# A two-layer graph network on one core: the gate's bias off TensorE, masks and output products in another order, first loads and products later

## The chip, the core and the metric

One core of a Trainium2 chip (trn2). The metric is the device time of one launch in microseconds, the median of several runs; lower is better. PE is TensorE, ACT ScalarE, DVE VectorE, POOL GpSimd, SP the engine that only issues transfers.

## The reference, cut to what matters

64 batches of 128 nodes with 384 features, `x` of 64 x 128 x 384, and a mask `adj` of 64 x 128 x 128. First a masked attention with 6 heads of 64, then a layer norm, then a graph attention with 12 heads of 32, a gate, and a second layer norm:

```python
# layer 0, per batch
q, k, v = x @ Wq + bq, x @ Wk + bk, x @ Wv + bv
probs = softmax(q k^T / 8 + where(mask, 0, -9e15))      # 6 heads
x1 = layernorm(x + (probs v) @ Wf + bf)
# layer 1, per batch
h = x1 @ W                                              # 12 heads
src, dst = tanh(h) . w_src, tanh(h) . w_dst
attn = softmax(where(adj, leaky_relu(src + dst^T), -999))
f = elu(attn h + b)
gate = sigmoid(x1 @ H_w^T + H_b)
out = layernorm(x1 + gate * f + (1 - gate) * x1)
```

## The kernel before, in words

Every projection is a split product (`split_product`, L250): both factors are held as a rounded high part and a remainder, and for each of the three chunks of 128 rows three products are added up (hi hi, lo hi, hi lo), so nine matmuls of 384 or 512 columns. In the trace all of them have line L254 and differ by tiles: `wq`, `wk`, `wv` (q, k, v of four batches at once), `wf` (output), `w` (h) and `hw` (gate). The gate's product ends with a tenth matmul (L429) that adds the bias: `ones_b` times `hb_rows`, in which the bias lies in three bf16 parts. ScalarE reads the finished sum from PSUM and stores the tangent of its half (L672); VectorE uses it two batches later (L846).

The work is written out by hand. Each engine has its own loop over 18 groups `n`, with four steps `j` each, and the order in the text is the order on the engine; semaphores tie them together. In a step three batches are under way: `ta` in the attention, `tl = ta - 2` in the first half of the graph layer ("gat"), `tl - 1` in its softmax and product ("tail"), and `tl - 2` in gating and second norm. Beside them the projections of the next group are made in four portions (`fill_a`, `fill_b`). "First batch" below is one with j = 0, "fourth batch" one with j = 3, in which v is projected. Group 0 has projections alone; group 16 has attention without projections; group 17 finishes the graph layer.

TensorE's step (L488 to L536): scores of `ta` (L355); turn f (L485); turn x1 (L410); a portion of projections; h; a second portion; turn p0 (L363); gate chunk 0; turn the exponentials of four heads (L467); context (L383); gate chunk 1; four more heads; gate chunk 2 and the bias (L429); output chunks 0 and 1; turn the six small columns `sd` (L435, L436); the last four heads; output chunk 2; the logits (L449), three matmuls in three banks of `ps_d`; the mask of the next batch's scores (L345), two bf16 matmuls into `ps_s`; the product with h (L477, "apply"). The logits wait for `rows_L` (ScalarE, L680) and `cols_R` (VectorE, L911).

VectorE's step, as far as it is near: copy p0T's odd half (L852), h with its bias (L860), the sums `sd` (L866), one evacuation of q, k or v, `ctxT_lo` (L747), then sd split into three bf16 parts by five small instructions (L892 to L902), a copy of four turned heads (L765), `cols_R` (L911), and the end of the second residual with its statistics (L920).

ScalarE's step: x1T_hi (L612), exponentials of the scores (L621), an evacuation, in fourth batches also the rounding of the next x (L558), elu's exponential (L638), tanh of h (L644), exponentials of heads 0 to 3 (L592), p0T's even half (L655), heads 4 to 7, ctxT_hi (L663), heads 8 to 11, the gate (L672), copies of turned heads (L604), rows_L, the three parts of z (L690), and fT (L696).

GpSimd's step: the mask added to z in three parts (L1000, up to batch 57; from batch 58 on TensorE adds it, L454, and VectorE sums the exponentials, L773), the multiply of p0 by the inverse sums (L1029), tanh(h) times the two weight rows (L1037), the two normalisations (L986 to L991), and two of x with bias (L978) or of the remainder of x (L945).

At the start SP issues x, four weights, the constants and two more weights, each weight into a staging buffer; ScalarE's queue issues the two small biases, the identity and the adjacency (1 MB, as bytes, turned into the bf16 `mask` by POOL, L962). After the projections of group 0 TensorE multiplies bv with Wf (`bias_product`, L323, in fp32), VectorE splits the gate's bias (L727 to L736), a transfer of POOL moves it to `hb_rows`, and VectorE adds bf to make `bf_all` (L881); the first mask of the scores waits for that.

## Time and profile before

| what | value |
|---|---|
| median of the runs shown | 1112.39 us (1108.36 to 1113.97, 3 runs) |
| the profiled execution | 1113.29 us |
| its span, first to last instruction | 1111.3 us |
| mean granted clock of TensorE | 0.986 |
| instructions | 25345 |

The profile is one execution. "Idle before" is the time that an engine stood still just before an instruction, with the name of what ended it. Matmuls are pipelined, so the time between the starts of two neighbours is what one costs, and its duration is longer. In timelines neighbours of one kind are merged, with their count behind an x.

### The profile page before, as it was taken

How to read it: one execution, taken by the hardware profiler on the slowest of the kernel's cores; microseconds unless marked ns; L12 is line 12 of the kernel's file. 1: busy time of each engine (PE TensorE's matmuls, PEld its weight loads, DVE VectorE, ACT ScalarE, POOL GpSimd, SP SyncE). 2: the span in 40 equal slices, each digit the busy share in tenths (PEclk: the TensorE clock that was granted, in tenths of full speed). 3: DMA queues.
4: the chain of work that ended last, by engine and by line, in shares of the span. 5: the costliest groups of instructions: out<-in, count | busy, mean ns of one | idle time of the engine just before them, and what ended most of it. 6: DMA issues, size and time to landing. Idle time of an engine off the chain costs nothing.

```text
span 1111.3 us, 25345 instructions
## 1 busy us (share of the span) xinstructions
PE 1055.4 (95%) x8318; PEld 883.4 (79%) x8318; DVE 916.6 (82%) x1844; ACT 878.1 (79%) x3183; POOL 748.0 (67%) x893
## 2 busy tenths in 40 slices
PE   5889999999999999999999999999999999997774
PEld 4678888888888888888888888888888888886552
DVE  4447888888888888888888888889888888988986
ACT  3348888888888888888888888888888888888754
POOL 1467777676777677677767768776776877665323
PEclk9999999999999999999999999999999999999986
DMA  9101002010200201020020102002020200100000
GB/s 273 59 2 58 16 9 73 16 65 16 71 17 9 72 15 65 16 72 17 9 73 15 65 16 72 16 8 73 16 71 10 72 15 9 44 16 15 9 15 29
DMA packets 25892, 44.65 MB, mean 40 GB/s; under 512 B 2462, under 2 KB 23714, under 8 KB 25762
## 3 DMA queue, kind: packets, MB, share of 16 engines
q1 hardware_dynamic: 23234, 41.91, 11.2%
q10 hardware_dynamic: 2496, 1.12, 0.5%
q8 instruction: 68, 1.11, 0.4%
q14 instruction: 62, 0.51, 0.2%
q0 software_dynamic: 32, 0.00, 0.0%
HBM read 30.43 MB, written 12.58 MB: 39 GB/s over the span
## 4 chain that ended last, share of the span: by engine, by line
PE 87%; issue 6%; POOL 4%; DVE 2%; ACT 1%; DMA 1%; POOLq 0%; ACTq 0%; DVEq 0%
PE ps_b L254 22%; PE ps_d L254 17%; PE ps_a L254 13%; PE ps_d L467 7%; PE ps_s L355 5%; PE ps_a L383 4%; PE ps_c L477 4%; PE ps_s L363 4%; PE ps_d L449 3%; PE ps_c L485 3%; PE ps_s L345 2%; PE ps_b L410 2%; POOL thw L1037 1%; PE ps_d L429 1%; POOL s L989 1%
## 5 line engine op out<-in xcount | busy, mean ns | idle before, releaser
L592 ACT ACTIVATE z<-z,s 128x128 f32<-128x128 f32 x696 | 270.0, 394 | 0.0
L1000 POOL TENSOR_TENSOR z<-z,mask 128x512 f32<-128x512 f32 x174 | 197.6, 1164 | 62.8 <-ACT z L690 62.8
L1029 POOL TENSOR_TENSOR p<-p,s 128x768 f32<-128x768 f32 x64 | 94.2, 1472 | 168.7 <-DVE s L823 168.7
L621 ACT ACTIVATE p<-ps_s,s 128x128 f32<-128x128 f32 x384 | 135.3, 374 | 12.0 <-DVE s L789 11.9
L592 ACT ACTIVATION_READ_ACCUMULATOR z<-z,s 128x1 f32 x696 | 135.3, 194 | 0.0
L1037 POOL TENSOR_TENSOR thw<-th,w_sd 128x768 f32<-128x768 f32 x64 | 117.6, 1837 | 18.7 <-ACT th L644 18.7
L467 PE MATMUL ps_d<-ident,z 128*128 128x128 f32 x768 | 117.6, 276 | 5.4 <-ACT z L595 5.2
L690 ACT ACTIVATE z<-ps_d 128x512 f32<-128x512 f32 x192 | 100.8, 597 | 25.7 <-PE ps_d L449 19.7
L467 PEld LDWEIGHTS ps_d<-ident,z 128*128 128x128 f32 x768 | 90.1, 142 | 13.0 <-ACT z L595 7.1
L852 DVE COPY p0T<-ps_s 128x384 f32<-128x384 f32 x64 | 35.7, 558 | 71.3 <-PE ps_s L363 71.3
L612 ACT ACTIVATE x1T_hi<-ps_b 128x384 fp32r<-128x384 f32 x64 | 31.5, 492 | 74.1 <-PE ps_b L410 74.1
L604 ACT ACTIVATE p1T<-ps_d 128x512 f32<-128x512 f32 x128 | 76.0, 594 | 14.4 <-PE ps_d L467 14.3
L254 PE MATMUL ps_d<-hw_hi,x1T_hi 128*128 128x384 f32 x192 | 82.1, 428 | 0.0
L621 ACT ACTIVATION_READ_ACCUMULATOR p<-ps_s,s 128x1 f32 x384 | 81.9, 213 | 0.0
L254 PE MATMUL ps_b<-wf_hi,ctxT_hi 128*128 128x384 f32 x192 | 78.6, 409 | 2.7 <-DVE ctxT_lo L747 1.3
L989 POOL TENSOR_TENSOR s<-s,minus_half 128x1 f32<-128x1 f32 x128 | 72.3, 565 | 10.7
L817 DVE TENSOR_REDUCE s<-z 128x8 f32<-128x1024 f32 x64 | 77.3, 1208 | 0.0
L254 PE MATMUL ps_d<-w_hi,x1T_hi 128*128 128x384 f32 x192 | 66.0, 344 | 7.0 <-DVE x1T_lo L747 7.0
L945 POOL TENSOR_TENSOR xT_lo<-x_cols,xT_hi 128x768 fp32r<-128x768 f32 x30 | 58.8, 1980 | 16.9 <-DVE sd_parts L902 9.4
L789 DVE TENSOR_REDUCE s<-ps_s 128x6 f32<-128x768 f32 x64 | 60.4, 944 | 10.6 <-PE ps_s L355 10.3
L978 POOL TENSOR_TENSOR xb<-xb,bf_all 128x768 f32<-128x768 f32 x32 | 58.5, 1828 | 11.9 <-DVE sd_parts L902 10.1
L254 PE MATMUL ps_d<-w_lo,x1T_hi 128*128 128x384 f32 x192 | 65.3, 340 | 0.0
(160 smaller groups left out, 3429.7 us busy)
## 6 DMA issues: line engine op xcount, KB each, us to landing
x_cols<-in_xT_dram SPq DMA_DIRECT2D x16, 768.0 KB, 6.3
xb<-in_x_dram SPq DMA_DIRECT2D x16, 768.0 KB, 4.9
out_dram<-y SPq DMA_DIRECT2D x64, 192.0 KB, 1.9
z<-in_L_gnn_Wq_dram SPq DMA_DIRECT2D x1, 576.0 KB, 6.9
p1T<-in_L_gnn_Wk_dram SPq DMA_DIRECT2D x1, 576.0 KB, 9.3
qT<-in_L_gnn_Wv_dram SPq DMA_DIRECT2D x1, 576.0 KB, 11.8
kT<-in_L_gnn_Wf_dram SPq DMA_DIRECT2D x1, 576.0 KB, 13.9
z<-in_L_gnn_W_dram SPq DMA_DIRECT2D x1, 576.0 KB, 12.1
```

The lines of the kernel that those rows point to most:

```text
L254: last = pe.matmul(out_ap, lhs(a, c), rhs(b, c), start=(c == 0 and k == 0), stop=(closed and c == C - 1 and k == 2))
L467: last = pe.transpose(ps_d[:, q, (a % 4) * N:(a % 4 + 1) * N], z[:, a, :], ident[:])
L592: done = act.activation(z[:, a, :], z[:, a, :], ACT.Exp, bias=neg1[:, a:a + 1], accum_out=sum1[:, a:a + 1])
L604: act.activation(p1T[:, 4 * q:4 * q + 4, :], ps_d[:, q, :].rearrange("p (a n) -> p a n", a=4), ACT.Copy).then_inc(S[f"p1T_{q}"], 1)
L621: last = act.activation(p0[:, o, i, :], ps_s[:, o, i * N:(i + 1) * N], ACT.Exp, bias=neg0[:, k:k + 1], accum_out=sum0[:, k:k + 1])
L690: act.activation(z[:, 4 * q:4 * q + 4, :], ps_d[:, q, :].rearrange("p (a n) -> p a n", a=4), ACT.Prelu, alpha=0.2).then_inc(S["z_ready"], 1)
L789: dve.tensor_reduce(neg0.rearrange("p (o i) -> p o i", o=2), ps_s[:, :, 0:C * N].rearrange("p o (i n) -> p o i n", i=C), AX_X, ALU.max, ne ...
L817: dve.tensor_reduce(neg1[:, 0:8], z[:, 0:8, :], AX_X, ALU.max, negate=True).then_inc(S["neg1_ready"], 1)
L989: pool.tensor_tensor(rs, ve, minus_half[:], ALU.pow).then_inc(S[small], 1)
L1000: pool.tensor_tensor(z[:, 4 * q:4 * q + 4, :], z[:, 4 * q:4 * q + 4, :], mask[:, t, :].unsqueeze(1).broadcast_to([P, 4, N]), ALU.add).then ...
L1029: pool.tensor_tensor(p0[:].rearrange("p o i n -> p (o i) n"), p0[:].rearrange("p o i n -> p (o i) n"), inv0.unsqueeze(2).broadcast_to([P, ...
L1037: pool.tensor_tensor(thw[:], th[:].unsqueeze(1).broadcast_to([P, 2, D]), w_sd[:], ALU.mult).then_inc(S["thw_ready"], 1)
```

## The change

- The gate's bias leaves TensorE. The matmul L429 goes, with `ones_b`, `hb_rows`, their splitting on VectorE and the transfer. The bias is loaded once as 128 equal rows (`hb_all`, 192 KB). ScalarE copies the gate's sum plain from PSUM; in the next step GpSimd adds the bias, behind its masks of z and ahead of the multiply of p0; then ScalarE takes the tangent, in place, ahead of p0T's even half.
- TensorE's order: the mask of the next batch's scores goes from behind the logits to before the output projection, and of that projection only chunk 0 stays before the turn of sd; chunks 1 and 2 follow the last turned heads.
- ScalarE's order: fT is made between the first and the second part of z, not behind the third.
- The bound from which VectorE sums the exponentials goes from batch 58 to 61; up to there ScalarE's exponentials bring their sums along. The masks stay where they were.
- At the start: the adjacency is issued by SP ahead of the fourth weight; `bias_product` comes behind the first scores and writes `ps_c`, and `bf_all` follows on VectorE behind the first maxima; the wait for it goes from the first mask to the first turn of sd. The bf16 identity is made a step earlier, and x of group 0 gets its bias behind the first multiply of p0.

```diff
 UNFILLED = G * (NG - 1) - LAG
+UNATTENDED = B - LAG - 1
...
             for n, name in enumerate(W_ORDER):
+                if n == 3:
+                    sp.dma_start(adj_u8, adj_dram).then_inc(S["adj_in"], 16)
...
-                    sp.dma_start(hb_row, Hb.rearrange("(o d) -> o d", o=1)).then_inc(S["const_in"], 16)
+                    sp.dma_start(hb_all[:], Hb.partition_broadcast(P)).then_inc(S["const_in"], 16)
...
-                        last = pe.matmul(ps_s[:, 0, 0:D], bv_col[:, c:c + 1].broadcast_to([P, P]),
+                        last = pe.matmul(ps_c[:, 0:D], bv_col[:, c:c + 1].broadcast_to([P, P]),
                                          w_parts["wf"][k][:, c, :].bitcast(F32), start=(c == 0 and k == 0),
                                          stop=(c == C - 1 and k == 1))
...
-                    pe.wait_ge(S["bf_ready"], 1)
...
             def project_gate(chunks):
 
-                split_product(ps_d[:, 2, 0:D], lambda a, c: x1T[a][:, c, :],
-                              lambda b, c: w_parts["hw"][b][:, c, :], chunks, closed=False)
+                last = split_product(ps_d[:, 2, 0:D], lambda a, c: x1T[a][:, c, :],
+                                     lambda b, c: w_parts["hw"][b][:, c, :], chunks)
                 if chunks[-1] == C - 1:
-
-                    pe.matmul(ps_d[:, 2, 0:D], ones_b[:], hb_rows[:], start=False, stop=True
-                              ).then_inc(S["gate_made"], 1)
+                    last.then_inc(S["gate_made"], 1)
 
             def turn_sd(t):
 
                 pe.wait_ge(S["sd3_ready"], t + 1)
+                if t == 0:
+                    pe.wait_ge(S["bf_ready"], 1)
                 pe.transpose(ps_rows, sd_rows, ident_b[:]).then_inc(S["sd_turned"], 1)
                 pe.transpose(ps_cols, sd_cols, ident_b[:]).then_inc(S["sd_turned"], 1)
 
             def logits(t):
 
                 pe.wait_ge(S["h_ready"], t + 1)
-                pe.wait_ge(S["gate_ready"], t + 1)
+                pe.wait_ge(S["gate_moved"], t + 1)
                 pe.wait_ge(S["rows_ready"], t + 1)
                 pe.wait_ge(S["cols_ready"], t + 1)
...
                         scores(g, 1 - par, j)
+                        if ta == 0:
+                            bias_product()
...
-                    if n == 0 and j == 3:
-                        bias_product()
...
-                    if att:
-                        project_out(ta, g, j, n, (0, 1))
-                    if gat:
-                        turn_sd(tl)
-                    if tail:
-                        turn_p1(tl - 1, gat, (2,))
-                    if att:
-                        project_out(ta, g, j, n, (2,))
-                    if gat:
-                        logits(tl)
                     if 0 <= ta and ta + 1 < B:
                         scores_mask(ta + 1)
+                    if att:
+                        project_out(ta, g, j, n, (0,))
+                    if gat:
+                        turn_sd(tl)
+                    if tail:
+                        turn_p1(tl - 1, gat, (2,))
+                    if att:
+                        project_out(ta, g, j, n, (1, 2))
+                    if gat:
+                        logits(tl)
                     if tail:
                         apply_p1(tl - 1, (j + 1) % 2, gat)
             pipeline(pe, iteration)
...
-            act.dma_start(adj_u8, adj_dram).then_inc(S["adj_in"], 16)
...
-                        if t < UNFILLED:
+                        if t < UNATTENDED:
...
+                def product_f(t):
+
+                    act.wait_ge(S["ph_made"], t + 1)
+                    if due(t):
+                        act.wait_ge(S["f_turned"], t)
+                    act.activation(fT[:], ps_c[:, 0:D].rearrange("p (c n) -> p c n", c=C),
+                                   ACT.Copy).then_inc(S["fT_ready"], 1)
...
+                    if tail:
+                        act.wait_ge(S["gate_biased"], tl)
+                        act.activation(gate[:, (tl - 1) % 3, :], gate[:, (tl - 1) % 3, :], ACT.Tanh,
+                                       scale=0.5).then_inc(S["gate_ready"], 1)
                     if att:
                         act.wait_ge(S["p0_turned"], ta + 1)
...
-                        act.activation(gate[:, tl % 3, :], ps_d[:, 2, 0:D], ACT.Tanh,
-                                       scale=0.5).then_inc(S["gate_ready"], 1)
+                        act.activation(gate[:, tl % 3, :], ps_d[:, 2, 0:D], ACT.Copy).then_inc(S["gate_moved"], 1)
...
                             act.activation(z[:, 4 * q:4 * q + 4, :], ps_d[:, q, :].rearrange("p (a n) -> p a n", a=4),
                                            ACT.Prelu, alpha=0.2).then_inc(S["z_ready"], 1)
-                    if tail:
-                        act.wait_ge(S["ph_made"], tl)
-                        if due(tl - 1):
-                            act.wait_ge(S["f_turned"], tl - 1)
-                        act.activation(fT[:], ps_c[:, 0:D].rearrange("p (c n) -> p c n", c=C),
-                                       ACT.Copy).then_inc(S["fT_ready"], 1)
+                            if q == 0 and tail:
+                                product_f(tl - 1)
+                    elif tail:
+                        product_f(tl - 1)
             pipeline(act, iteration)
...
+                    if ta == 0:
+                        dve.wait_ge(S["bvf_made"], 1)
+                        dve.tensor_tensor(bf_all[:], ps_c[:, 0:D], bf_in, ALU.add).then_inc(S["bf_ready"], 1)
...
+                        dve.wait_ge(S["gate_ready"], t2 + 1)
...
+                    if n == 0 and j == 2:
+                        dve.wait_ge(S["ident_in_ready"], 16)
+                        dve.tensor_copy(ident_b[:], ident[:]).then_inc(S["consts_ready"], 1)
                     if n == 0 and j == 3:
                         small_constants()
-                        dve.wait_ge(S["bvf_made"], 1)
-                        dve.tensor_tensor(bf_all[:], ps_s[:, 0, 0:D], bf_in, ALU.add).then_inc(S["bf_ready"], 1)
                     if att:
...
-                pool.wait_ge(S["hb_small"], 5)
-                pool.wait_ge(S["padding_ready"], 1)
-                pool.dma_start(hb_rows[0:3, :], hb_split[:]).then_inc(S["hb_moved"], 16)
...
                     if tail:
                         z_mask(tl - 1)
+                    if tail:
+                        pool.wait_ge(S["gate_moved"], tl)
+                        if tl == 1:
+                            pool.wait_ge(S["const_in"], 16 * 7)
+                        pool.tensor_tensor(gate[:, (tl - 1) % 3, :], gate[:, (tl - 1) % 3, :], hb_all[:], ALU.add
+                                           ).then_inc(S["gate_biased"], 1)
...
                     if ta == 0:
+                        xb_with_bias(0, 0, slice(0, 2))
+                        xb_with_bias(0, 0, slice(2, 4))
                         moved_constants()
...
-                    if n == 0 and j == 3:
-                        xb_with_bias(g, par, slice(0, 2))
-                        xb_with_bias(g, par, slice(2, 4))
```

## Rows read from the trace of the kernel before

**Rows 1.** Page, busy time of each engine over the span.

```profile
PE 1055.4 (95%) x8318; PEld 883.4 (79%) x8318; DVE 916.6 (82%) x1844; ACT 878.1 (79%) x3183; POOL 748.0 (67%) x893
```

**Rows 2.** Timeline of PE, one batch (start, duration, engine, line, operation, tiles, count, idle before).

```profile
574.69 0.34 PE L254 MATMUL ps_d<-hw_lo,x1T_hi 128*128 128x384 f32 x1
574.87 0.34 PE L429 MATMUL ps_d<-hb_rows,ones_b 128*128 128x384 bf16 x1
...
575.21 0.33 PE L254 MATMUL ps_b<-wf_hi,ctxT_lo 128*128 128x384 f32 x1
...
576.10 0.22 PE L435 MATMUL ps_c<-ident_b,sd_parts 128*96 128x128 bf16 x1
...
577.00 0.34 PE L254 MATMUL ps_b<-wf_lo,ctxT_hi 128*128 128x384 f32 x1
577.35 0.54 PE L449 MATMUL ps_d<-cols_R,rows_L 32*128 32x512 bf16 x3
577.82 0.50 PE L345 MATMUL ps_s<-mask,ident_b 128*128 128x384 bf16 x2
578.25 0.86 PE L477 MATMUL ps_c<-p1T,h 128*32 128x128 f32 x24
```

**Rows 3.** Timeline of DVE, the same batch.

```profile
575.72 0.18 DVE L902 CAST sd_parts<-sd_rest 128x24 bf16<-128x24 f32 x1
...
576.41 0.69 DVE L911 TENSOR_TENSOR cols_R<-ps_a,of_slot 96x512 bf16<-96x512 bf16 x1
```

**Rows 4.** Waits over the span (total, times, longest).

```profile
POOL p L1029 <- DVE s L823: 168.7, 64, 9.4
...
ACT p0T L655 <- PE ps_s L363: 40.6, 50, 2.2
```

**Rows 5.** Timeline of all engines, a fourth batch.

```profile
604.32 0.85 ACT L558 ACTIVATE xT_hi<-x_cols 128x768 fp32r<-128x768 f32 x1 [0.78 <-PE ps_b L254]
...
605.07 0.48 ACT L655 ACTIVATE p0T<-ps_s 128x384 f32<-128x384 f32 x1
...
605.78 0.88 PE L383 MATMUL ps_a<-p0T,v 128*64 128x128 f32 x12
...
607.56 0.56 DVE L747 TENSOR_TENSOR ctxT_lo<-ps_a,ctxT_hi 128x384 fp32r<-128x384 f32 x1 [0.30 <-ACT ctxT_hi L663]
...
608.09 0.66 POOL L991 TENSOR_SCALAR x<-r,s 128x384 f32<-128x384 f32 x1
...
608.24 0.55 DVE L894 TENSOR_TENSOR sd_rest<-sd,sd_parts 128x24 f32<-128x24 f32 x1
...
609.25 0.18 DVE L902 CAST sd_parts<-sd_rest 128x24 bf16<-128x24 f32 x1
```

**Rows 6.** Timeline of DVE, an earlier fourth batch: the cast at the same place.

```profile
90.88 0.61 DVE L892 CAST sd_parts<-sd 128x24 bf16<-128x24 f32 x1
```

**Rows 7.** Timeline of POOL, a first batch, and its multiply of the next.

```profile
613.41 3.41 POOL L1000 TENSOR_TENSOR z<-z,mask 128x512 f32<-128x512 f32 x3
617.36 1.47 POOL L1029 TENSOR_TENSOR p<-p,s 128x768 f32<-128x768 f32 x1 [0.54 <-DVE s L823]
```

**Rows 8.** Timeline of PE, the start of the attention.

```profile
32.23 0.81 PE L329 MATMUL ps_s<-wf_hi,bv_col 128*128 128x384 f32 x2
...
37.41 0.48 PE L345 MATMUL ps_s<-mask,ident_b 128*128 128x384 bf16 x2 [1.14 <-DVE bf_all L881]
...
43.84 0.88 PE L363 MATMUL ps_s<-ident,p 128*128 128x128 f32 x6 [0.78 <-POOL p L1029]
...
47.66 0.41 PE L254 MATMUL ps_b<-wf_hi,ctxT_hi 128*128 128x384 f32 x1 [1.29 <-issue]
```

**Rows 9.** Timeline of DVE, the start: the fifth weight.

```profile
23.47 1.23 DVE L718 CAST w_hi<-z 128x1152 fp32r<-128x1152 f32 x1 [0.63 <-DMA z<-in_L_gnn_W_dram]
```

**Rows 10.** Timeline of PE, a batch without projections.

```profile
1028.79 0.40 PE L449 MATMUL ps_d<-cols_R,rows_L 32*128 32x512 bf16 x3 [0.18 <-issue]
```

**Rows 11.** Timeline of ACT, the three parts of z and what follows fT.

```profile
577.76 1.57 ACT L690 ACTIVATE z<-ps_d 128x512 f32<-128x512 f32 x3 [0.31 <-PE ps_d L449]
...
580.83 0.49 ACT L612 ACTIVATE x1T_hi<-ps_b 128x384 fp32r<-128x384 f32 x1 [1.11 <-PE ps_b L410]
```

**Rows 12.** Busy time by stretch, the end (PE, PEld, DVE, ACT, POOL, PEclk, DMA share, GB/s).

```profile
1074.00:1084.00 10.00, 7.92 (x45) 5.86 (x43) 6.52 (x13) 4.36 (x10) 0.65 (x1) 0.51 0.00 0
```

More of the change, by code:

```diff
@@ L87, in build_program @@
         w_sd = sb("w_sd", [P, 2, D])
-        hb_rows = sb("hb_rows", [P, D], BF16)
+        hb_all = sb("hb_all", [P, D])
         mask = sb("mask", [P, B, N], BF16)
@@ L522, in iteration @@
                         project_gate((2,))
+                    if 0 <= ta and ta + 1 < B:
+                        scores_mask(ta + 1)
                     if att:
-                        project_out(ta, g, j, n, (0, 1))
+                        project_out(ta, g, j, n, (0,))
                     if gat:
@@ L902, in iteration @@
                         dve.tensor_copy(part[2], sd_rest[:, 1]).then_inc(S["sd3_ready"], 1)
-                    if tail and tt >= UNFILLED:
+                    if tail and tt >= UNATTENDED:
                         sum_exponentials(tt, 0)
@@ L913, in iteration @@
                                           ).then_inc(S["cols_ready"], 1)
-                    if tail and tt >= UNFILLED:
+                    if tail and tt >= UNATTENDED:
                         sum_exponentials(tt, 1)
```

37 lines of the change are left out of this document (8 added, 29 removed).

## The prediction

> **What bounds the kernel now.** I read the page first: PE is busy for 95% of the span, DVE 82%, ACT 79%, POOL 67% [rows 1]. One would take PE for the bound and every product saved for time saved. So the next view is PE's timeline of one batch in the steady part, beside DVE's. The reader is to look at starts, since a matmul's 0.34 is mostly pipeline: neighbours of 384 columns start 0.17 to 0.18 apart. PE runs without a gap except at one place: the last product of the output projection starts at 577.00, the logits could follow at 577.18, and they start at 577.35 [rows 2]. They wait for cols_R, which DVE ends at 577.10 [rows 3]. DVE is busy without a gap from the copy of p0T (L852) to there. So PE is the bound from the transposes of p0 onwards and again after the logits; between them, DVE's chain p0T, h, sums, evacuation, ctxT_lo, five small splits, cols_R is almost level with it. The batches repeat with a period of 15.6 us (first, second and third of a group of four) and about 17.75 us (fourth to first).
>
> **The removed bias product.** It costs PE 0.52 - 0.35 = 0.17 us: from the last gate product at 574.69 to the second output product at 575.21 there are 0.52, where two more products would be 0.35 [rows 2]. Over 64 batches that would be 11 us, if nothing else waited.
>
> **The new order on PE.** The two mask products cost 0.43 behind the logits (577.82 to 578.25), of which 0.32 are 2 x 384 columns; the other 0.11 is the passage from bf16 to the fp32 products, which now follows the logits directly. Ahead of the output projection they cost 2 x 0.17 = 0.34. Of that projection only one chunk (three products, 0.53) is ahead of the turn of sd instead of two. PE reaches the turn 0.17 - 0.34 + 0.53 = 0.36 earlier than 576.10, so at 575.74. But DVE ends the last split at 575.72 + 0.18 = 575.90 [rows 3], and PE can start some 0.05 later, at 575.95. The turn is thus only 0.15 earlier: **DVE's splits take the place of cols_R as the wait.** From the turn to the logits there were 1.08 without the gap (576.10 to 577.18), and now one chunk more, 1.61: logits at 577.56, after cols_R (577.10) and no longer waiting for it. The following apply (L477) comes 0.47 + 0.11 later, at 578.14 instead of 578.25. The gain in a second or third batch is 0.11 to 0.13 us, not the 0.17 + 0.17 = 0.34 that PE alone would give.
>
> **ScalarE's extra tangent** is one operation of 128x384: 0.48 long, the next one starting 0.10 before its end, so 0.38 per batch. In three batches of four ACT waits 0.70 us for the transposes of p0, and the tangent is hidden there (over the kernel that wait sums to 40.6 us in 50 batches) [rows 4]. In the fourth it is not: ACT waits for the v product instead, then rounds x (L558) and takes up p0T at 605.07 with no idle time before it, 0.15 after DVE [rows 5]. The tangent goes right between. p0T's even half then ends at 605.93 instead of 605.55; the context product (605.78) starts about 0.3 later; ctxT_hi comes 0.38 later, and ctxT_lo on DVE starts at 607.93 instead of 607.56. The first split then comes at 608.41, inside GpSimd's normalisation (608.09 to 608.75).
>
> Here the trace shows a collision: the split at 608.24 took 0.55, until GpSimd's operation ended, where its kind takes 0.18 [rows 5]. That the cast before it is held too is shown by an earlier batch, 0.61 for 0.17 [rows 6]. I let the cast wait until 608.79; the last split ends at 609.65 instead of 609.43, +0.22; in the batches in which it now ends 0.18 earlier it is +0.40. I take +0.31 for the turn of sd and, less 0.02 from the order, **+0.29 per fourth batch**. The Trainium skill (SBUF — State Buffer, on who interferes with whom) says that the pair of ports shared by VectorE and GpSimd is an exclusive lock for the whole instruction, for operations with two SBUF inputs or in a two-port mode. If only the two-input split were held and not the cast, the split would be released at the same 608.79 as now and the fourth batch would lose nothing.
>
> **GpSimd's extra add** isn't in the trace. Its nearest row is the mask addition, 3 of 128x512 in 3.41, 1.13 each [rows 7]; three quarters of that is 0.85. From below, a one-input operation of 128x384 takes 0.66 [rows 5]; from above 1.13. It stands before the multiply of p0, for which POOL waits in all 64 batches, 168.7 us in sum [rows 4], least in a first batch: 0.54 [rows 7]. There the multiply comes 0.3 later; 617.36 + 1.47 + 0.3 = 619.13 is still 0.7 ahead of PE's transposes (7.34 after the scores at 612.47). But POOL's later normalisation also comes 0.3 later and holds DVE's last split instead of the one before: the turn of sd stays where it was, and a first batch gains 0. In no other batch is it seen.
>
> **Sum over the 14 groups of the steady part:** 0 - 0.12 - 0.12 + 0.29 = +0.05 each; I take **0**.
>
> **The start.** PE now does six bias products from 32.23 to 36.1, then idles until 37.41, because DVE splits the gate's bias into three and only then makes bf_all. Afterwards come mask, scores (1.28 together) and the first fill. In the new order mask and scores start at 32.2 and the 3.9 us of bias products hide the softmax: the fill starts 1.3 earlier, the wait of 0.78 before the transposes goes, and the mask product hides in the wait of 1.29 before the output projection (0.43), in the second batch again (0.43) [rows 8]. With 0.4 for the third and fourth batch that is -3.3. The adjacency moves from ACT's queue to SP's ahead of the fourth weight, and the bias becomes a broadcast of 192 KB instead of 1.5: DVE already waits 0.63 for the fifth weight [rows 9], and a later one delays k and PE. The first weights come earlier, so I charge +0.3, between -0.5 and +2. GpSimd adds the xb bias (two of 1.83) after p0, long before it is read. **Start: -3.0.**
>
> **The drained part** (four batches without projections, period 15.45) is a chain of latencies. The logits wait 0.18 there too, at 13.26 after the scores at 1015.53 [rows 10]; sums of exponentials leave DVE, the mask leaves the chain: -0.35, -0.53, -0.53, -0.39, **-1.8**. Three last batches: the tangent lies before the last transposes once (+0.38), two bias products are gone (-0.34): **0**.
>
> **The exchange of z and fT on ACT.** fT is now made after the first of three z's, which start about 0.5 apart (three in 1.57) [rows 11], but it waits for the apply product, which ends near 579.05. z's third part so ends about 1.3 later, near 580.6; ACT was idle 1.11 before 580.83, so it fits; without that cover the exponentials of attention would come later by what exceeds it. POOL's masks in a second batch end at 582.4 and the add at 583.3, before the multiply at 583.94.
>
> **Sum:** -3.0 + 0 - 1.8 + 0 = -4.8 against the profiled execution's 1113.29 us (span 1111.3 and 2.0 around it): 1108.5. That execution is 0.9 above the median of the runs shown, 1112.39; I predict 1108.5 us, 0.35% below that median. This measurement can hardly tell less than 0.5%, 5.6 us, from nothing.
>
> **Rivals.** (1) *The DVE chain gives way* (36%): if the cast is not held in the fourth batch (-0.31) or the last split slips through in the first (up to -0.35), a group gains 0.35 to 0.9 and the time is 1096 to 1104. At its far end PE alone decides: 56 x 0.34 = 19 us and 5 at the ends, 1089. For it: PE has no other wait. Against: in the rows DVE has no slack to give. By the lock as the Trainium skill states it, whoever starts first holds the pair, and the cast may or may not be in a mode that needs it; the two cases lie 0.31 x 14 = 4.3 us apart. (2) *GpSimd becomes late in first batches* (12%). The add and DVE's two-input operations hold each other, and it takes about 2 us instead of 0.85. The multiply of p0 then ends 1.4 late, at 620.3, after PE wants it (619.81), and th's product (L1037) and the sums on DVE behind it as well: about 1.0 per group, 14 us, 1108.5 + 14 = 1122. It decides from an add of 1.5 us on (0.54 of wait and 0.9 of lead used up). For it: two-input operations do meet there. Against it: the masks of twice its columns keep to 1.13 in the same place. (3) *The gain at the start is eaten by the later loads* (10%): the fifth weight 3 us late, 1111.5. (4) The clock: at the end 10 us ran at a granted 0.51, the 1.2 GHz level, after PE had waited on DVE and ACT [rows 12]; if that stretch moves, 3 us of PE's work there change by half, so 2 to 3 us either way; it widens the range of every case.
>
> **Numbers.** The forecast case has 42%, its own range 1104 to 1113; a quarter of it lies under 1106.8. Faster by over 0.5%: 0.9 x 36 + 10 = 42. Slower by over 0.5%: 12. Within: 46. The range leaves out the far end of the first rival and most of the second: 1098 to 1115.
>
> **What would show it.** In the changed profile: the turn of sd right behind DVE's last split and the logits no longer 0.25 behind cols_R; periods near 15.5 for second and third batches, 17.9 or more from the fourth to the first; ACT's p0T copy 0.38 later in fourth batches only; the add near 0.85; scores at 32.6 instead of 37.8. Periods of 15.3 and 17.4 would prove the first rival right and my DVE chain wrong; PE waiting for POOL before the transposes of p0 in the steady part, the second.

## The result and the profile after

| | before | after |
|---|---|---|
| median of six runs each, us | 1110.51 (1108.07 to 1113.97) | 1101.91 (1100.91 to 1103.01) |
| ratio after to before | | 0.9923 (95%: 0.9901 to 0.9944) |
| the profiled execution and its span, us | 1113.29, 1111.3 | 1102.09, 1100.3 |
| mean granted clock | 0.986 | 0.989 |

The change makes the kernel 0.8% faster. The forecast was 1108.5, 4.8 us under the profiled execution of before; it came out 11.2 under it (8.6 by the medians: the profiled execution of before is 2.8 above its kernel's median). So the time lies in the range, but the gain is more than twice the one that the steps gave, and it came from elsewhere: 1101.9 is below the forecast case's own 1104 and inside the first rival's 1096 to 1104. A table of the scores' starts shows where. I group the 64 batches by their place in the group of four; a period is the time from one batch's first score to the next one's, averaged over batches 8 to 58 of the one profiled execution. The last three rows and the one of the fifth batch add up to the whole.

| | forecast | before | after | difference |
|---|---|---|---|---|
| first score of all | 32.6 | 37.82 | 37.09 | -0.73 |
| first score of the fifth batch | -3.0 | 95.39 | 95.83 | +0.44 |
| first batch, period | 0 | 15.63 | 15.27 | -0.36 |
| second | -0.12 | 15.61 | 15.34 | -0.27 |
| third | -0.12 | 15.62 | 15.42 | -0.20 |
| fourth | +0.29 | 17.76 | 17.93 | +0.17 |
| fifth to 61st batch, sum | 0 | 904.72 | 895.05 | -9.67 |
| 61st to 64th (drained; the forecast is for four periods, these are three) | -1.8 | 46.33 | 45.58 | -0.75 |
| from the last score on | 0 | 64.9 | 63.8 | -1.0 |

+0.44, -9.67, -0.75 and -1.0 make -11.0, what the spans differ by. Nearly all came from the steady part, for which the forecast was nothing; the start, for which it was -3.0, brought nothing.

The 95.39 of before is not a clean number. From 61 to 64 us of its span the granted clock was 0.53; the second and third periods are 13.05 and 15.03, where a kernel with the same start (the product off alone, below) has 11.96 and 14.60 at 1.00, and reaches the fifth batch at 93.97. Against about 94 the changed start is some 1.9 us slower, not 0.4.

From the page after: the busy times, and the group of the new add (partitions x elements, count, busy, mean ns, idle before).

```profile
PE 1040.9 (95%) x8254; PEld 874.7 (79%) x8254; DVE 900.6 (82%) x1830; ACT 909.5 (83%) x3282; POOL 812.3 (74%) x954
...
L1024 POOL TENSOR_TENSOR gate<-gate,hb_all 128x384 f32<-128x384 f32 x64 | 68.0, 1062 | 0.7 <-ACT gate L680 0.7
```

PE has lost 14.5 us of work and is busy for 95% as before [rows 1]; that share told nothing of the gain. The add takes 1.06 in the mean, not 0.85.

The waits after (total, times, longest):

```profile
POOL p L1028 <- DVE s L819: 82.2, 50, 8.3
...
PEld ps_c L432 <- DVE sd_parts L900: 19.5, 47, 1.5
...
ACT p0T L663 <- PE ps_s L361: 16.4, 46, 2.2
```

The second line is the wait that the forecast named: PE at the turn of sd now waits for DVE's last split in 47 batches. POOL has half its slack before the multiply left (82.2 us in sum, where it was 168.7), and ACT 0.36 instead of 0.81 each before p0T, the room that the tangent took [rows 4].

**A second batch after**, the same one as in [rows 2, 3, 11]; its scores began at 558.85. First PE, then DVE, POOL and ACT (start, duration, engine, line).

```profile
571.34 0.26 PE L432 MATMUL ps_c<-ident_b,sd_parts 128*96 128x128 bf16 x1
...
573.08 0.39 PE L446 MATMUL ps_d<-cols_R,rows_L 32*128 32x512 bf16 x3
573.40 0.86 PE L474 MATMUL ps_c<-p1T,h 128*32 128x128 f32 x24
```

```profile
570.62 0.45 DVE L897 TENSOR_TENSOR sd_rest<-sd_rest,sd_parts 128x24 f32<-128x24 f32 x1
571.11 0.18 DVE L900 CAST sd_parts<-sd_rest 128x24 bf16<-128x24 f32 x1
...
571.80 0.68 DVE L909 TENSOR_TENSOR cols_R<-ps_a,of_slot 96x512 bf16<-96x512 bf16 x1
```

```profile
570.38 0.66 POOL L984 TENSOR_SCALAR x<-r,s 128x384 f32<-128x384 f32 x1
```

```profile
573.50 0.60 ACT L697 ACTIVATE z<-ps_d 128x512 f32<-128x512 f32 x1 [0.77 <-PE ps_d L446]
574.33 0.49 ACT L600 ACTIVATE fT<-ps_c 128x384 f32<-128x384 f32 x1 [0.23 <-PE ps_c L474]
```

The turn of sd (571.34) follows the last split (571.11 + 0.18) by 0.05, as forecast, and cols_R is done at 572.48, 0.60 before the logits: it is no longer the wait. The fourth of DVE's five small operations is held until POOL's normalisation ends (570.38 + 0.66). What differs from the forecast stands behind the turn. The logits come 1.74 after it, not 1.61: the last output product starts at 572.81, and from it to the bf16 logits there are 0.27 where I had counted 0.17. The apply comes 0.32 after the logits, not 0.58.

**A first batch after**, scores at 607.54: POOL, DVE.

```profile
611.95 1.02 POOL L1024 TENSOR_TENSOR gate<-gate,hb_all 128x384 f32<-128x384 f32 x1
...
619.60 0.66 POOL L984 TENSOR_SCALAR x<-r,s 128x384 f32<-128x384 f32 x1
```

```profile
619.53 0.18 DVE L900 CAST sd_parts<-sd_rest 128x24 bf16<-128x24 f32 x1
```

The add moves POOL's whole sequence back, and its normalisation now begins 0.07 after the last split has begun: the split is through in 0.18. The turn of sd then starts at 619.82, 12.28 after the scores, against 12.49 in a second batch.

**A fourth batch after**, scores at 589.61, all engines, beside [rows 5]:

```profile
599.28 0.85 ACT L554 ACTIVATE xT_hi<-x_cols 128x768 fp32r<-128x768 f32 x1 [0.78 <-PE ps_b L253]
600.03 0.51 ACT L657 ACTIVATE gate<-gate 128x384 f32<-128x384 f32 x1
600.45 0.47 ACT L663 ACTIVATE p0T<-ps_s 128x384 f32<-128x384 f32 x1
...
601.02 0.88 PE L381 MATMUL ps_a<-p0T,v 128*64 128x128 f32 x12 [0.21 <-issue]
...
602.93 0.56 DVE L740 TENSOR_TENSOR ctxT_lo<-ps_a,ctxT_hi 128x384 fp32r<-128x384 f32 x1 [0.70 <-ACT ctxT_hi L671]
603.04 0.67 POOL L984 TENSOR_SCALAR x<-r,s 128x384 f32<-128x384 f32 x1
603.40 0.34 DVE L890 CAST sd_parts<-sd 128x24 bf16<-128x24 f32 x1
...
604.42 0.18 DVE L900 CAST sd_parts<-sd_rest 128x24 bf16<-128x24 f32 x1
```

The tangent lies before p0T, the context begins 0.28 later than before (11.40 after the scores instead of 11.12, means of the fourth batches), and the cast at 603.40 is held to 603.74, when POOL's operation has ended. The last split is done 14.99 after the scores instead of 14.68: the +0.31 of the forecast.

**The start after**: SP's issues, then DVE, then PE, then the window from 31.0 on (PE, PEld, DVE, ACT, POOL, PEclk, DMA share, GB/s).

```profile
3.19 0.83 SPq L198 DMA_DIRECT2D x<-in_adj_dram  x1
4.06 11.93 SPq L209 DMA_DIRECT2D kT<-in_L_gnn_Wf_dram  x1
...
19.41 0.43 SPq L209 DMA_DIRECT2D z<-in_L_gnn_W_dram  x1
```

```profile
27.42 0.76 DVE L723 CAST w_hi<-z 128x1152 fp32r<-128x1152 f32 x1 [4.08 <-DMA z<-in_L_gnn_W_dram]
...
29.49 0.74 DVE L750 TENSOR_SCALAR kT<-ps_b,bk_col 128x512 f32<-128x512 f32 x1
```

```profile
30.29 0.44 PE L253 MATMUL ps_b<-wv_hi,xT_hi 128*128 128x384 f32 x1 [2.07 <-DVE kT L750]
...
37.09 0.94 PE L353 MATMUL ps_s<-kT,qT 64*128 64x128 f32 x12
```

```profile
31.00:34.40 3.40, 3.40 (x13) 3.40 (x12) 1.99 (x3) 0.85 (x1) 0.42 (x1) 0.50 0.13 54
```

The issue of Wf (the fourth weight), the next on SP's queue behind the adjacency, lasts 11.93 us, and what follows it is issued 6 to 12 us later than before: the fifth weight (W, staged in z) reaches DVE 4 us later [rows 9], DVE's evacuation of k stands behind it, PE waits 2.07 for that, and after the gap it runs 3.4 us at a granted 0.50, the 1.2 GHz level (its products start 0.32 apart instead of 0.17); from 34.4 on it is back at full clock. The first score comes at 37.09 instead of the 32.6 forecast.

### The profile page after: what moved, and what is told of

Read it like the earlier page. It is cut to its first block, busy times and chain, and to the rows that moved or that the text cites. A ratio compares the mean times of both kernels' runs of the same rounds, so it can differ in the third digit from the quotient of the medians.

```text
span 1100.3 us, 25365 instructions
## 1 busy us (share of the span) xinstructions
PE 1040.9 (95%) x8254; PEld 874.7 (79%) x8254; DVE 900.6 (82%) x1830; ACT 909.5 (83%) x3282; POOL 812.3 (74%) x954
## 4 chain that ended last, share of the span: by engine, by line
PE 75%; DVE 10%; issue 8%; POOL 4%; SPq 2%; ACT 1%; DMA 1%; POOLq 0%; DVEq 0%
PE ps_b L253 20%; PE ps_d L253 13%; PE ps_a L253 13%; PE ps_d L464 5%; PE ps_s L353 5%; PE ps_c L474 4%; PE ps_s L361 4%; PE ps_c L482 3%; DVE sd L863 2%; PE ps_a L381 2%; PE ps_b L408 2%; PE ps_d L446 2%; DVE kT L750 2%; DVE h L857 1%; DVE sd_rest L897 1%
## 5 line engine op out<-in xcount | busy, mean ns | idle before, releaser
L588 ACT ACTIVATE z<-z,s 128x128 f32<-128x128 f32 x732 | 284.4, 399 | 0.0
L1028 POOL TENSOR_TENSOR p<-p,s 128x768 f32<-128x768 f32 x64 | 94.2, 1473 | 82.2 <-DVE s L819 82.2
L697 ACT ACTIVATE z<-ps_d 128x512 f32<-128x512 f32 x192 | 107.5, 599 | 51.4 <-PE ps_d L446 45.0
L625 ACT ACTIVATE p<-ps_s,s 128x128 f32<-128x128 f32 x384 | 135.0, 374 | 12.7 <-DVE s L782 11.2
L588 ACT ACTIVATION_READ_ACCUMULATOR z<-z,s 128x1 f32 x732 | 145.0, 198 | 0.0
L1024 POOL TENSOR_TENSOR gate<-gate,hb_all 128x384 f32<-128x384 f32 x64 | 68.0, 1062 | 0.7 <-ACT gate L680 0.7
L253 PE MATMUL ps_d<-w_lo,x1T_hi 128*128 128x384 f32 x192 | 65.7, 342 | 0.0
```

What stands on the lines that cost most here:

```text
L253: last = pe.matmul(out_ap, lhs(a, c), rhs(b, c), start=(c == 0 and k == 0), stop=(closed and c == C - 1 and k == 2))
L588: done = act.activation(z[:, a, :], z[:, a, :], ACT.Exp, bias=neg1[:, a:a + 1], accum_out=sum1[:, a:a + 1])
L625: last = act.activation(p0[:, o, i, :], ps_s[:, o, i * N:(i + 1) * N], ACT.Exp, bias=neg0[:, k:k + 1], accum_out=sum0[:, k:k + 1])
L697: act.activation(z[:, 4 * q:4 * q + 4, :], ps_d[:, q, :].rearrange("p (a n) -> p a n", a=4), ACT.Prelu, alpha=0.2).then_inc(S["z_ready"], 1)
L1024: pool.tensor_tensor(gate[:, (tl - 1) % 3, :], gate[:, (tl - 1) % 3, :], hb_all[:], ALU.add).then_inc(S["gate_biased"], 1)
L1028: pool.tensor_tensor(p0[:].rearrange("p o i n -> p (o i) n"), p0[:].rearrange("p o i n -> p (o i) n"), inv0.unsqueeze(2).broadcast_to([P, ...
```

## The experiments

All periods below are means of the profiled execution over batches 8 to 58, as in the table. Two kernels leave part of the work out: e3_product_off_only and e8_no_bias_at_all compute the gate without its bias. Ratios are to the kernel before, run on the same chip.

**The adjacency back on ScalarE's queue.** Everything else as after.

```diff
-                if n == 3:
-                    sp.dma_start(adj_u8, adj_dram).then_inc(S["adj_in"], 16)
...
+            act.dma_start(adj_u8, adj_dram).then_inc(S["adj_in"], 16)
```

> The changed kernel with the adjacency's transfer back on ScalarE's queue, behind the identity. Queue theory (the gain that I forecast at the start was lost because the transfer of 1 MB in small packets held up SP's queue, 11.9 us at the fourth weight, and so the fifth weight, x of the next group and PE behind them): 4 us less than the changed kernel, 1098, the first scores at about 32.6 us of the span instead of 37.09, and nothing else moves. Rival (the bias product between scores and fill, or the order of VectorE's work, costs the start its gain): within 1 us of the changed kernel.

Measured: 1098.67 (1096.80 to 1100.61), ratio 0.9886 (0.9862 to 0.9911). SP's queue and PE:

```profile
3.07 0.52 SPq L207 DMA_DIRECT2D kT<-in_L_gnn_Wf_dram  x1
...
11.20 0.38 SPq L207 DMA_DIRECT2D z<-in_L_gnn_W_dram  x1
```

```profile
32.96 0.94 PE L351 MATMUL ps_s<-kT,qT 64*128 64x128 f32 x12
```

The issue of Wf takes 0.52, the fifth weight is in at 23.65, the first score comes at 32.96, 4.1 earlier, and the steady part is the same (895.42 from the fifth to the 61st batch). So it was the place of this one transfer, and not the broadcast of the bias, which is still there.

The 4.1 are two things. Three other kernels of this section leave the adjacency on SP's queue, and there the same issue lasts 11.51 (a product back), 11.11 (mask behind) and 11.33 (fT behind). PE's gap before the v products is 3.13, 2.64 and 2.92. In the last two the clock does not fall behind it, and the first score comes at 34.56 and 35.16; in the first it falls as in the changed kernel, and the score comes at 36.90. So the late weight alone costs about 2 us, and the other 2 are the clock, which falls in some executions and not in others; which ones isn't explained by the length of the gap.

Of the 4.1, 2.8 are left at the fifth batch (93.05): here the granted clock fell to 0.63 in a stretch of the second batch (59 to 62 us), and its period is 13.26 instead of 11.99. The Trainium skill (Perfetto Trace Analysis, DMA Optimizations) says that where the issuing engine's track is full of DMA slices, spreading the issues over several engines may help; by that rule the move to SP was the wrong direction, and the 11.93 of one issue against 0.52 agrees.

**A product back at the gate's end.** After, with a tenth bf16 matmul of zeros, so that PE's load at the gate is that of before.

```diff
                 if chunks[-1] == C - 1:
+                    pe.matmul(ps_d[:, 2, 0:D], ones_b[:], zero_rows[:], start=False, stop=True
+                              ).then_inc(S["gate_made"], 1)
```

> The changed kernel with a tenth matmul (bf16, zeros) back at the end of the gate's product, so that PE does again what the change took off it. Chain theory (in second, third and fourth batches PE waits for VectorE's last split before it turns sd, so a product ahead of it is free): +2 us, only first batches (0.1 each) and the four without projections pay. PE theory (the engine that is 95% busy pays for every product): 64 x 0.17 = +11 us.

Measured: 1100.20 (1099.56 to 1100.69), ratio 0.9906 (0.9886 to 0.9925), the same as the changed kernel within the intervals; periods 15.27, 15.36, 15.42, 17.94.

```profile
570.31 0.34 PE L427 MATMUL ps_d<-zero_rows,ones_b 128*128 128x384 bf16 x1
...
571.40 0.26 PE L435 MATMUL ps_c<-ident_b,sd_parts 128*96 128x128 bf16 x1
...
573.15 0.39 PE L449 MATMUL ps_d<-cols_R,rows_L 32*128 32x512 bf16 x3
```

The product costs nothing in the new order. In this second batch (scores at 558.89) the turn is 12.51 after the scores, where it was 12.49 without it: it waits for the split either way. So the matmul, after which the change is named, is not where the gain is.

**The product off alone.** The kernel before without L429 and with nothing in its place.

```diff
-                    pe.matmul(ps_d[:, 2, 0:D], ones_b[:], hb_rows[:], start=False, stop=True
-                              ).then_inc(S["gate_made"], 1)
+                    last.then_inc(S["gate_made"], 1)
```

> The kernel before with the gate's bias product left out and nothing else changed: it computes the gate without its bias. Chain theory (the logits wait for cols_R, whose chain on VectorE hangs on the transposes of p0, which lie ahead of the product): 0 to -1 us against before. PE theory: -11 us.

Measured: 1108.05 (1103.89 to 1109.28), ratio 0.9970 (0.9956 to 0.9983); periods 15.52, 15.49, 15.52, 17.76. In the old order the product is worth about 0.1 in three batches of four, and 1.9 to 4.9 us in all, more than the 0 to 1 expected. The logits stay at 13.90 to 13.93 after the scores (13.93 to 13.96 before), behind cols_R, as the forecast read it; most of the 0.1 comes after them:

```profile
573.44 0.44 PE L447 MATMUL ps_d<-cols_R,rows_L 32*128 32x512 bf16 x3
573.81 0.50 PE L345 MATMUL ps_s<-mask,ident_b 128*128 128x384 bf16 x2
```

Here the mask follows the first logits matmul by 0.37; in before by 0.47 [rows 2]. The three logits matmuls write three banks, and the third one's bank is free only when ScalarE has copied the last turned heads from it. That copy comes earlier by what the turn comes earlier. In before the copy, and the third matmul when the window is made narrow enough to part it from the other two (which start at 577.35):

```profile
576.85 0.60 ACT L604 ACTIVATE p1T<-ps_d 128x512 f32<-128x512 f32 x1 [0.23 <-PE ps_d L467]
```

```profile
577.50 0.39 PE L449 MATMUL ps_d<-cols_R,rows_L 32*128 32x512 bf16 x1
```

The copy ends at 577.45, the third matmul starts 0.05 later and 0.15 behind the first two. In before 0.15 of the stretch behind the logits was this wait; the merged row hides it.

**The order alone.** The kernel before with the new order on PE (mask before the output projection, chunks 1 and 2 behind the last heads); **the mask put back**: after, with the mask behind the logits; **fT put back**: after, with fT behind the third part of z.

```diff
+                    if 0 <= ta and ta + 1 < B:
+                        scores_mask(ta + 1)
                     if att:
-                        project_out(ta, g, j, n, (0, 1))
+                        project_out(ta, g, j, n, (0,))
...
-                        project_out(ta, g, j, n, (2,))
+                        project_out(ta, g, j, n, (1, 2))
```

> The kernel before with TensorE's new order alone (mask ahead of the output projection, one chunk before the turn of sd, two behind), bias product and everything else as before. Chain theory: apply comes 0.26 earlier in a batch as in the changed kernel, since the bias product is hidden, but fT, made behind three parts of z that now start 0.35 later, is late for its turn by 0.3 to 0.4 and takes that back: between -4 and +5 us against before. If fT isn't in the way: -14 us. PE theory (order is nothing, the removed product all): 0.

> The changed kernel with the mask of the next scores back behind the logits; the output projection stays split one chunk and two. Chain theory: ahead of the turn of sd the mask was hidden in PE's wait for VectorE, behind the logits it is bare, 0.32 of columns and about 0.1 of passage, 0.44 from logits to apply: 60 x 0.4 = +25 us against the changed kernel (1127). PE theory (the same products cost the same anywhere): within 2 us of it.

> The changed kernel with fT made behind the third part of z again, as before. Theory from the order-only run (fT ended 17.1 after the scores there, and the turn of f started 0.05 later): fT is about 0.95 later than in the changed kernel, its turn 0.7 later, and a period grows by 0.4 to 0.6: +20 to +30 us. Rival (the order-only run is slower for another reason, the bias product or the tangent): within 3 us of the changed kernel.

| | median | ratio | first, second, third, fourth |
|---|---|---|---|
| order only | 1122.83 (1119.53 to 1124.86) | 1.0107 (1.0080 to 1.0134) | 15.87, 15.84, 15.80, 17.95 |
| mask behind | 1126.66 (1124.13 to 1128.65) | 1.0142 (1.0119 to 1.0164) | 15.82, 15.77, 15.77, 18.36 |
| fT behind | 1126.35 (1124.84 to 1130.76) | 1.0153 (1.0125 to 1.0181) | 15.83, 15.79, 15.78, 18.37 |

ACT and PE of the order alone, from a second batch to a third (scores at 585.54):

```profile
584.85 1.57 ACT L690 ACTIVATE z<-ps_d 128x512 f32<-128x512 f32 x3 [0.77 <-PE ps_d L449]
586.30 0.51 ACT L696 ACTIVATE fT<-ps_c 128x384 f32<-128x384 f32 x1
```

```profile
586.86 0.55 PE L485 MATMUL ps_c<-ident,fT 128*128 128x128 f32 x3 [0.38 <-ACT fT L696]
```

With the mask gone from behind the logits, the apply and the scores come 0.57 earlier after the logits, but ScalarE's three z's still take 1.45 before fT, and PE stands 0.38 before it turns f. The wait of PE on fT is new; in before the mask's 0.43 hid it. So the new order is worth nothing alone, it costs 12 us (expected were -4 to +5); and the exchange on ScalarE is what lets it pay. The mask put back instead loses about 0.4 per batch, its own 0.43 behind the logits, without the second output chunk ahead of the turn that it had in before. The order without the exchange, and the exchange without the mask's new place, are each slower than the kernel before.

**The gate's bias stays on PE.** The new order and the exchange on ScalarE; bias, loads and start as before.

> The kernel before with two changes of order alone: TensorE's new order and fT behind the first part of z. The bias product, its splitting, the tangent from PSUM and the whole start stay as before. Chain theory (the gain is the order's, and the product was hidden): periods 15.42, 15.34, 15.41 and 17.68, as in the run without any bias, a steady part of about 893.5 us and in all 1110.5 - 11.3 - 1.5 = 1098, less than the changed kernel's 1101.9. PE theory: the 11 us of products come back on top of the changed kernel, 1107 or more.

Measured: 1098.72 (1094.96 to 1099.60), ratio 0.9869 (0.9849 to 0.9889); periods 15.43, 15.35, 15.41, 17.59; steady part 892.67. This is below the changed kernel: 3.0 us of it at the fifth batch (92.87), where the adjacency doesn't hold up SP, and 2.4 in the steady part. Against it the changed one wins 0.16 in a first batch (the split that is not held) and loses 0.34 in a fourth; the next runs put 0.26 of that down to the tangent, the rest isn't explained. The profiled execution is the fastest of its six, and the median is that of the changed kernel with the adjacency moved back (1098.67). So in the way the change does it, taking the bias off TensorE bought nothing.

**No bias at all.** After with the adjacency on ScalarE's queue and with neither add nor second tangent.

> The changed kernel with the adjacency on ScalarE's queue and without the gate's bias: ScalarE makes the tangent from PSUM as before, GpSimd adds nothing; it computes the gate without its bias. It prices the bias's new home. Chain theory: the tangent is hidden in three batches and costs the fourth: fourth batches 17.94 to 17.5, first to third unchanged within 0.05 but for the first, where VectorE's last split meets GpSimd's normalisation again (up to +0.3); 3 to 6 us less than the run with the adjacency alone moved (1098.7). Rival (GpSimd's 64 adds of 1.06 cost time everywhere): periods of all batches shorter, 10 us or more.

Measured: 1095.16 (1094.12 to 1096.51), ratio 0.9860 (0.9843 to 0.9877); periods 15.42, 15.34, 15.41, 17.67. Two of them tell something. The fourth is back at 17.67: the tangent was its loss. The first is at 15.42, 0.15 worse than with the add; POOL and DVE of a first batch beginning at 601.10:

```profile
612.68 0.68 POOL L980 TENSOR_SCALAR x<-r,s 128x384 f32<-128x384 f32 x1
```

```profile
612.86 0.53 DVE L893 TENSOR_TENSOR sd_rest<-sd_rest,sd_parts 128x24 f32<-128x24 f32 x1
613.43 0.18 DVE L896 CAST sd_parts<-sd_rest 128x24 bf16<-128x24 f32 x1
```

Without the add POOL is earlier and DVE's fourth small operation, begun 0.18 after POOL's, is held to its end. The add, which costs POOL 68 us over the kernel, gains PE 0.15 in each first batch by moving a collision past DVE's last split.

**The tangent later.** After with the adjacency on ScalarE's queue, in two places: just before the gate's plain copy, and in the idle time before z.

```diff
-                    if tail:
-                        act.wait_ge(S["gate_biased"], tl)
-                        act.activation(gate[:, (tl - 1) % 3, :], gate[:, (tl - 1) % 3, :], ACT.Tanh,
-                                       scale=0.5).then_inc(S["gate_ready"], 1)
                     if att:
                         act.wait_ge(S["p0_turned"], ta + 1)
```

> The changed kernel with the adjacency on ScalarE's queue and the tangent moved behind the exponentials of heads 8 to 11. Chain theory: in fourth batches p0T's even half, the context and ctxT_hi are no longer 0.3 to 0.4 late, so the fourth period falls from 17.94 to about 17.55: 5 us less than 1098.7, unless the gate's copy, the rows and the last turned heads, now 0.38 later, reach the logits or apply (they have 0.1 to 0.3 to spare in the others): then up to +0.15 in three of four batches, which gives the 5 us back.

> The changed kernel with the adjacency on ScalarE's queue and the tangent behind the copies of the turned heads, right ahead of the first part of z, where ScalarE stood still for 0.77 us in the changed kernel. Chain theory: the fourth batch gets its context at 11.13 and its last split at 14.76, its period falls from 17.94 to about 17.68, the other three keep 15.27, 15.36 and 15.42: 14 x 0.26 = 3.6 us less than 1098.7, 1095. The miss of the run with the tangent behind heads 8 to 11 (the gate's copy came late and the last turn of heads waited for it) can't come here, since the copy is ahead. Rival (z comes late for GpSimd's masks or the product h): second and third periods 0.1 to 0.3 longer, 1099 or more.

Before the copy: 1112.21 (1111.09 to 1114.32), ratio 1.0012 (1.0000 to 1.0025); periods 15.68, 15.69, 15.69, 17.93. ACT and PE of a second batch beginning at 561.35:

```profile
573.35 0.52 ACT L672 ACTIVATE gate<-gate 128x384 f32<-128x384 f32 x1
573.76 0.47 ACT L679 ACTIVATE gate<-ps_d 128x384 f32<-128x384 f32 x1
```

```profile
573.93 0.22 PE L431 MATMUL ps_a<-ident_b,sd_parts 128*96 128x128 bf16 x1
574.29 0.66 PE L462 MATMUL ps_d<-ident,z 128*128 128x128 f32 x4
```

The last heads are turned into the bank that holds the gate's sum. They wait for its copy (573.76 + 0.47), start 0.36 behind the turn's second matmul instead of 0.06, and all behind them is 0.3 late, where up to 0.15 was expected. This wait was overlooked: TensorE waits for the copy here, so a tangent ahead of the copy delays it.

In the idle 0.77 before z: 1095.63 (1094.83 to 1096.10), ratio 0.9847 (0.9829 to 0.9866); periods 15.28, 15.35, 15.42, 17.67. In a fourth batch (scores at 583.26):

```profile
599.39 0.51 ACT L687 ACTIVATE gate<-gate 128x384 f32<-128x384 f32 x1
600.25 0.60 ACT L696 ACTIVATE z<-ps_d 128x512 f32<-128x512 f32 x1 [0.36 <-PE ps_d L444]
```

The tangent is hidden in all four, the context is back at 11.13 after the scores, and the first batch keeps its 15.28. With the adjacency's place mended too, this kernel does the whole computation and is faster than both.

**The sums' bound back at 58**, on top of the last:

```diff
-UNATTENDED = B - LAG - 1
+UNATTENDED = UNFILLED
```

> The kernel of the first run of this call with the bound of the sums back at batch 58: VectorE sums the exponentials of batches 58 to 60 again. Only batches 61 to 63 can move, and I expect cols_R 0.6 later behind the first sum, the logits by up to 0.3: 0.5 to 1 us more in all, in the drained periods and nowhere else. Rival: the drained part's gain is all the order's, and this is within 0.2 us.

Measured: 1092.76 (1091.31 to 1095.14), ratio 0.9827 (0.9800 to 0.9853), the lowest of all, where 0.5 to 1 us more was expected. The intervals of this one and the last overlap, so that it is better is not shown. The three drained periods, which alone were to move, are the same (45.58 and 45.60 in sum). In the profiled executions this kernel and the last reach the last scores within 0.6 (1027.98 and 1028.56), and the rest takes 62.7 and 65.7. There the clock differs; a window of the tangent-last kernel and the same one of this kernel (columns as above, 0.61 and 1.00 is the granted clock; in the eight us behind it 0.50 and 0.61 against 0.57 and 1.00):

```profile
1056.00:1060.00 4.00, 3.05 (x30) 1.38 (x30) 2.49 (x6) 1.29 (x4) 1.06 (x2) 0.61 0.00 0
```

```profile
1056.00:1060.00 4.00, 2.22 (x34) 1.32 (x31) 2.14 (x6) 2.54 (x5) 0.01 (x1) 1.00 0.02 4
```

The times of the single executions go with the clock: this kernel took 1091.31 at a mean granted 0.995, 1092.46 at 0.991, 1093.06 at 0.989 and 1095.14 at 0.986, and the last one, at 0.986 to 0.988 in all five, 1094.83 to 1096.10. At the same clock the two can't be told apart. Whether VectorE's sums have a part in where the clock falls stays open.

## Why the prediction was right, and where not

**How far it was luck.** The measured time lies in the range of 1098 to 1115, but no part of the sum came out at its forecast. Against the steps the steady part came out 9.7 us faster, the start 3.4 slower, the drained part about 1 slower and the end 1 faster. Errors of opposite sign met, and the time landed where the first rival (36%) had put it.

**Right.** That PE's saved product gives way to a wait (the turn of sd at DVE's last split + 0.05) is in the rows of second, third and fourth batches (in a first one PE comes to the turn 0.10 after the split), and the product put back showed that it is free. The fourth batch: the tangent not hidden, the context 0.28 late, the cast held, the split +0.31; the forecast said +0.29 for the period, measured were +0.17, since the gain behind the logits (below) is in it too. That the cast is held and not only the two-input split was the choice on which the first rival's first half hung; 603.40 shows it held. The Trainium skill (SBUF — State Buffer, Who interferes with whom) says that whichever of the two engines starts first has the pair of ports for the whole instruction: the three collisions above all go by who began first, and by the row at 603.40 the cast is among the operations that are held. The exchange of z and fT fitted (x1T_hi idle 0.17 before it in the second batch), and POOL's add disturbed no later batch.

**The steady part, forecast 0, measured -9.7.** Two terms failed, both small and multiplied by 14 or 56.
- *"The following apply comes 0.47 + 0.11 later"*: 0.58 from logits to apply. It was measured as 0.32. The 0.11 was to be added for a passage from the logits to the fp32 apply; nothing is added (0.32 to the apply here, 0.33 to the bf16 mask with the mask put back, 584.14 to 584.47). And of the 0.47, 0.15 was the third logits matmul waiting for ScalarE to empty its bank: the product off alone leaves 0.37, the mask put back 0.33. The row showed it: 0.54 for three matmuls [rows 2], where they take 0.39 now. Against that, the way from turn to logits was 1.74, not 1.61. Net 0.13 to 0.16 more per second batch than forecast: -0.27 for -0.12.
- *"A first batch gains 0"*: the normalisation was to hold the last split. The add takes 1.06, 0.2 more than the estimate, and the normalisation begins 0.07 behind the split's start; with an add of 0.85 it would, by this working, have begun just before it. This is the second half of the first rival, priced at up to -0.35; measured -0.36 with the other term in it, and 0.15 of it goes when the add goes.

I had given the chain 0 to lose or win and listed periods of 15.3 (with 17.4 in the fourth) as proof that the DVE chain was wrong. The periods are 15.27 to 15.42 (and 17.93), and the chain was right: the sign chosen was not specific to the theory, since any gain behind the logits gives it as well.

**The start, forecast -3.0, measured +0.4.** The failed term is the charge of +0.3, between -0.5 and +2, for the later loads. I took the transfer's bytes as the cost, and not that the next issue on the same queue may stand behind it for 11.93 us. With the adjacency on the old queue the first score is at 32.96 against the 32.6 forecast. The fifth batch then comes at 91.11 with the tangent last (90.56 to 91.11 in the four kernels whose clock stays up there), which is 2.9 before the undisturbed 93.97 of the product off alone, with the old order and start. So the other terms of the start came out nearly as summed, and rival 3 (3 us, 10%) came true at the start; the steady part covered it up.

**The drained part, -1.8 in four periods, measured -0.75 in three**, 0.23 to 0.26 each instead of 0.35 to 0.53. The failed term is that the logits would come earlier: they come 13.33 after the scores, before 13.26 [rows 10], and only the way from them to the apply is shorter. There ScalarE now makes the sums of the exponentials, and the gate's copy comes late (ACT, then PE, after):

```profile
1017.23 0.47 ACT L680 ACTIVATE gate<-ps_d 128x384 f32<-128x384 f32 x1
```

```profile
1017.76 0.66 PE L464 MATMUL ps_d<-ident,z 128*128 128x128 f32 x4
```

The last heads wait for it (1017.23 + 0.47) and start 0.19 behind the second matmul of the turn (1017.57) instead of 0.06: again the wait on the copy. But that is not the whole reason: with VectorE's sums put back, where the copy is early, cols_R is late instead, and the three periods are the same. The end's -1.0 is of the size of what the clock does there and isn't explained.

## What to carry to other kernels

A change of several parts is read by undoing each part in the full change and by doing each alone: here the part that gave it its name was worth nothing, two others lost 24 to 25 us each when undone singly, and the whole got faster when the adjacency went back to its queue. Where something is moved out from between two others, look in the duration of the merged row for a wait that has no row: three matmuls in 0.54 that elsewhere take 0.39 are a wait. Before a stretch of one profile is taken for the effect of a change, look at its granted clock in both: here some 1.5 us of the start of before were that. And price a moved transfer by the queue that it is put on, not by its bytes.

## What the runs showed of the hardware

- One issue behind the adjacency's transfer on SP's queue lasted 11.93 us (11.11 to 11.93 in the four kernels that have it there); the same issue 0.52 when that transfer was on ScalarE's queue. ScalarE issued nothing behind it, so no run shows whether an issue would have stood there as long.
- One of VectorE's splits of sd (128x24) is held by GpSimd's normalisation if it begins after it (0.18 after: 0.53 long; 0.24 after: 0.45; 0.36 after: 0.34), each to about its end, and not at all if it begins 0.07 before. So a later GpSimd can make TensorE faster.
- GpSimd's add of 128x384 in fp32 takes 1.06 us (64 of them), 1.6 times its one-input operation of that size (0.66) [rows 5].
- After a gap of 2.07 us PE ran 3.4 us at a granted 0.50 in the first projections, in a place where the kernel before and the one with the adjacency moved back stayed at 1.00. After gaps of 2.64 and 2.92 at the same place (mask behind, fT behind) it stayed at 1.00 too.
- Times of one kernel go roughly with its mean granted clock: of eleven executions of the kernel before on one chip, the two at 0.993 took 1108.94 and 1109.23 us, the four at 0.986 took 1112.92 to 1114.79 (and one at 0.992 took 1112.49).
